# Two attention stages with their loops written out, fewer stack transfers, and new orders for SP and POOL

## What is computed

```python
x = x + attn(layernorm(x))        # 16 heads of width 16, relative positions
x = x + ffn(layernorm(x))         # a transformer layer: attention, then top-2 of 8 experts

# attn: distance of every query and key, clipped at +-64, picks a row of embK / embV
logits = einsum('bhqd,bhkd->bhqk', q, k) + einsum('bhqd,qkd->bhqk', q, embK[idx])
w = softmax(logits)
out = einsum('bhqk,bhkd->bhqd', w, v) + einsum('bhqk,qkd->bhqd', w, embV[idx])

# ffn, its attention: no relative positions
h = layernorm(x) * g + b
attn = softmax(q @ k.T / sqrt(16));  x = x + (attn @ v) @ w_o + b_o
# then layernorm, gate, and two of eight experts with 1024 hidden units a token
```

## Time and profile before

| | |
|---|---|
| median of 3 runs | 4886.3 us (4877.15 to 4907.61) |
| profiled execution | 4905.31 us, its span 4903.5 us |
| mean granted TensorE clock | 0.897 of full |
| relative attention, first to last collected head | 366.46 to 2376.10 us |
| plain attention, the same | 2749.21 to 4181.90 us |
| busy over the span | PE 85%, DVE 75%, ACT 61%, POOL 30% |

### The profile page before, as it was taken

The page is one execution under the profiler, slowest core; times in us unless marked ns, Lnnn a source line. Parts: engine busy times, 40 slices in busy tenths (PEclk is TensorE's granted clock), DMA queues, the critical chain, the costliest instruction groups (busy, mean ns, idle before and its releaser), DMA issues. The chain is left out here.

```text
span 4903.5 us, 90470 instructions
## 1 busy us (share of the span) xinstructions
PE 4163.6 (85%) x26888; PEld 2168.5 (44%) x26888; DVE 3684.1 (75%) x6647; ACT 3011.5 (61%) x5838; POOL 1451.2 (30%) x1418
## 2 busy tenths in 40 slices
PE   3769898989989898989655999999999999669997
PEld 1434444444444444444333333333333333469997
DVE  2678777787877777777357888888888888557775
ACT  0217777677767676767211578778778778236665
POOL 0025555465655555555300000000000000333332
PEclk9959998898989898989777899999999999779999
DMA  3656666566656666656545323223233322566664
GB/s 99 230 106 158 143 144 143 136 153 142 155 133 151 137 150 142 149 126 149 162 149 168 49 41 47 39 42 47 40 42 44 47 39 40 140 200 175 175 175 118
DMA packets 512569, 579.13 MB, mean 118 GB/s; under 512 B 71976, under 2 KB 451928, under 8 KB 502000
## 3 DMA queue, kind: packets, MB, share of 16 engines
q1 hardware_dynamic: 453568, 489.90, 44.7%
q10 hardware_dynamic: 38656, 58.73, 3.2%
q0 software_dynamic: 19824, 24.52, 3.2%
HBM read 365.10 MB, written 210.95 MB: 117 GB/s over the span
## 5 line engine op out<-in xcount | busy, mean ns | idle before, releaser
L1325 ACT ACTIVATE ra_p<-ra_psS 128x512 f32<-128x512 f32 x2051 | 1106.9, 604 | 565.7 <-PE ra_psS L1398 465.6
L633 DVE TENSOR_REDUCE pa_pm<-pa_psA 128x2 f32<-128x1024 f32 x1068 | 1261.6, 1220 | 175.5 <-PE pa_psA L724 175.3
L1232 DVE TENSOR_REDUCE ra_pm<-ra_psA 128x1 f32<-128x896 f32 x1072 | 1165.8, 1088 | 236.6 <-PE ra_psA L1358 179.8
L698 ACT ACTIVATE pa_p<-pa_psS 128x512 f32<-128x512 f32 x2054 | 1068.4, 602 | 287.3 <-PE pa_psS L747 264.9
L1358 PE MATMUL ra_psA<-ra_zs,ra_qs 48*128 48x512 f32 x2144 | 833.7, 479 | 179.7 <-DVE ra_rst L1251 113.5
L747 PE MATMUL pa_psS<-pa_qs,pa_zs 50*128 50x512 f32 x2056 | 807.5, 471 | 96.0 <-ACT pa_p L698 81.9
L724 PE MATMUL pa_psA<-pa_zs,pa_qs 48*128 48x512 f32 x2136 | 839.0, 477 | 50.5 <-DVE pa_recb L664 29.9
L1398 PE MATMUL ra_psS<-ra_qs,ra_zs 50*128 50x512 f32 (+3 forms) x2182 | 781.5, 439 | 48.4 <-ACT ra_p L1325 43.3
L747 PEld LDWEIGHTS pa_psS<-pa_qs,pa_zs 50*128 50x128 f32 x2056 | 349.0, 188 | 658.6 <-ACT pa_p L698 618.3
L1429 PE MATMUL ra_psO<-ra_p,ra_vs 128*32 128x512 f32 (+3 forms) x6400 | 600.9, 482 | 0.0
L1398 PEld LDWEIGHTS ra_psS<-ra_qs,ra_zs 50*128 50x128 f32 x2182 | 378.4, 200 | 451.2 <-ACT ra_p L1325 319.2
(11 more groups left out here) (250 smaller groups left out, 5295.2 us busy)
## 6 DMA issues: line engine op xcount, KB each, us to landing
relative_rows<-ra_rst SPq DMA_DIRECT2D x136, 512.0 KB, 5.1
ra_blk<-window_rows SPq DMA_DIRECT2D x128, 512.0 KB, 4.6
mo_w_raw<-ffn_W SPq DMA_DIRECT2D x58, 1024.0 KB, 5.6
ra_dl<-relative_rows SPq DMA_DIRECT2D x136, 256.0 KB, 4.2
window_rows<-ra_pc SPq DMA_DIRECT2D x128, 256.0 KB, 5.2
pa_qs<-q_halves SPq DMA_DIRECT2D x210, 128.0 KB, 5.6
pa_zs<-kl_halves SPq DMA_DIRECT2D x210, 128.0 KB, 6.9
ra_qs<-q_halves SPq DMA_DIRECT2D x204, 128.0 KB, 4.4
```

Source lines behind the costliest of these rows:

```text
L633: dve.reduce_max(pm[:, par, 2 * a:2 * a + 2], psA[w][:, :, :], AX.X).then_inc(s_am.h, 1)
L698: act.activation(pr[:, i % NPR, :], psS[:, slot(i), :], ACT.Exp).then_inc(s_ex.h, 1)
L1232: dve.reduce_max(pm[:, q, i, 2 * left:2 * left + 1], psA[w][:, lo:lo + 2 * G - P], AX.X).then_inc(s_far.h, 1)
L1325: act.activation(dst, psS[:, slot(i), :], ACT.Exp if kind == "E" else ACT.Copy).then_inc(s_cp.h, 1)
```

## The change

Four things change. In both attention stages the loops of SP, POOL, DVE and ACT are written out (all heads, waits on constants); the first pair of lines below stands for eight such pairs. `load_stack` uses five transfers for the same bytes, its rows in another order (the high and low rows of the keys alternate), for which `k_halves` holds both sides of the keys in one tensor and `e_stack` has the same order. `gather_denominators` uses one transfer for four, and the table `k_side` two for sixteen. SP's and POOL's orders in the relative stage are laid out anew, with other constants.

```diff
-            with sp.Fori(0, HEADS // U) as it:
+            for it in range(HEADS // U):
...
-for _c, _at in reversed(tuple(enumerate((38, 50, 59, 98)))):
+for _c, _at in reversed(tuple(enumerate((38, 53, 83, 88)))):
...
-WX_STEPS = (9, 10, 10, 10, 11, 11, 12, 13, 13, 15, 17, 18, 18, 18, 19, 20)
+WX_STEPS = (8, 10, 10, 10, 12, 13, 13, 14, 14, 14, 15, 17, 21, 22, 22, 23)
-REL_AHEAD, REL_LEAD = 16, 6
+REL_AHEAD, REL_LEAD = 18, 7
-RC_REL = 32
-SUM_TURNS = (8, 15, 24, 27)
+RC_REL = 30
+SUM_TURNS = (10, 17, 23, 28)
...
+                sp.dma_start(qs[at:two, w, :].bitcast(F32), bass.AP(qd.tensor, q0, [[T, DK], [0, 2], [1, S]])
+                             ).then_inc(done[w].h, 16)
+                sp.dma_start(qs[two:last, w, :].bitcast(F32), bass.AP(qd.tensor, q0 + D * T, [[T, DK], [1, S]])
+                             ).then_inc(done[w].h, 16)
+                for side in range(2):
+                    sp.dma_start(zs[at:two, w, side * far:(side + 1) * far].bitcast(F32),
+                                 bass.AP(kd.tensor, k0 + side * (D * T - 64), [[T, DK], [2 * D * T, 2], [1, far]])
+                                 ).then_inc(done[w].h, 16)
+                sp.dma_start(zs[two:last, w, 0:2 * far].bitcast(F32).rearrange("r (s c) -> r s c", s=2),
+                             bass.AP(kd.tensor, k0, [[T, DK], [D * T - 64, 2], [1, far]])).then_inc(done[w].h, 16)
...
+                sp.dma_start(den_d.rearrange("u (c q) -> c u q", c=4), ob[DK:P:32, :, :]).then_inc(s_dw.h, 16)
+                s_dw.wait(sp, 16 * (n + 1))
...
                 for p in range(U):
-                    load_stack(t + 1, p + 1, 64, s_qe, STEPS * t)
+                    if p == 2:
+                        load_v(t + 2, 4 * (t + 2))
                     write_r(t + 2, p, 0)
+                    write_r(t + 2, p, 1)
                     write_p(t, p, 0)
-                    write_r(t + 2, p, 1)
+                    write_p(t, p, 1)
                     read_p(t, p, 0)
                     read_r(t + 2, p, 0)
-                    write_p(t, p, 1)
+                    load_stack(t + 1, p + 1, 64, s_qe, STEPS * t)
+                    read_r(t + 2, p, 1)
                     write_r(t + 2, p, 2)
                     read_p(t, p, 1)
                     write_r(t + 2, p, 3)
-                    if p == 2:
-                        load_v(t + 2, 4 * (t + 2))
-                    read_r(t + 2, p, 1)
-                    read_r(t + 2, p, 3)
+                    write_p(t, p, 3)
                     write_p(t, p, 2)
                     if p % 2 == 0:
                         gather_denominators(t, n)
-                    write_p(t, p, 3)
+                    read_r(t + 2, p, 2)
                     read_p(t, p, 2)
-                    read_r(t + 2, p, 2)
+                    read_p(t, p, 3)
+                    read_r(t + 2, p, 3)
                     send_m(t + 1, p + 1)
-                    read_p(t, p, 3)
+                    if p % 2 == 0:
+                        spread_reciprocals(n)
                     s_am.wait(sp, 32 * (t + 2))
                     load_stack(t + 3, p + 1, 0, s_qa)
-                    if p % 2 == 0:
-                        spread_reciprocals(n)
                     if p % 2 == 0:
                         store_o(t, n)
...
                     t, n = U * it + p, 2 * it + p // 2
-                    lay_v(t + 1, p + 1, it + 1 + (p + 1) // U)
                     join_p(t, p, 0)
                     join_p(t, p, 1)
+                    lay_v(t + 1, p + 1, it + 1 + (p + 1) // U)
+                    fold_p(t, 0)
                     part_r(t + 2, 0)
-                    fold_p(t, 0)
                     join_p(t, p, 2)
                     join_p(t, p, 3)
+                    part_r(t + 2, 1)
                     fold_p(t, 1)
-                    part_r(t + 2, 1)
+                    part_r(t + 2, 2)
                     fold_p(t, 2)
                     fold_p(t, 3)
-                    part_r(t + 2, 2)
...
-                for hh in range(P // DK):
-                    sp.dma_start(k_side[hh * DK:(hh + 1) * DK, side:side + 1],
-                                 emb_k[r:r + 1, :].rearrange("r (d a) -> (r d) a", a=1)).then_inc(s_ld, 16)
+                row = emb_k[r:r + 1, :]
+                sp.dma_start(k_side[:, side:side + 1],
+                             bass.AP(row.tensor, row.offset, [[0, P // DK], [1, DK], [1, 1]])).then_inc(s_ld, 16)
```

More of the change, by code:

```diff
@@ L617, in _ @@
             lay_v(0, 0)
-            with pool.Fori(0, HEADS // U) as it:
+            for it in range(HEADS // U):
                 for p in range(U):
@@ L670, in _ @@
                     split_m(0, n % 2)
-            with dve.Fori(0, HEADS // U) as it:
+            for it in range(HEADS // U):
                 for p in range(U):
@@ L707, in _ @@
                 exp(0, i)
-            with act.Fori(0, HEADS // U) as it:
+            for it in range(HEADS // U):
                 for p in range(U):
@@ L933, in rel_attention @@
         blk = ctx.enter_context(nc.Block())
-        NLD = 16 * (len(Q2) + 2 * len(K2))
+        NLD = 16 * 5
         NINIT = 7
@@ L989, in load_stack @@
                 w = p % 2
-                row, col, col64 = ready(sp, h * DK), ready(sp, b * S), ready(sp, b * S + 64)
                 if free is not None:
                     s_us.wait(sp, free)
[L993 to L998, removed]
+                q0, k0 = qd.offset + h * DK * T + b * S, kd.offset + h * DK * T + b * S + 64
+                far, two, last = S - 64, at + 2 * DK, at + PR
+                sp.dma_start(qs[at:two, w, :].bitcast(F32), bass.AP(qd.tensor, q0, [[T, DK], [0, 2], [1, S]])
[8 more added lines that the diff above has]
+                             bass.AP(kd.tensor, k0, [[T, DK], [D * T - 64, 2], [1, far]])).then_inc(done[w].h, 16)
             def load_v(t, laid):
@@ L2412, in dram @@
         return nc.dram_tensor(name, shape, dt).ap()
-    q2, kl2, kr2 = (dram(n, (NP2, D, T)) for n in ("q_halves", "kl_halves", "kr_halves"))
+    q2 = dram("q_halves", (NP2, D, T))
+    k_sides = dram("k_halves", (NP2, 2, D, T))
+    kl2, kr2 = k_sides[:, 1, :, :], k_sides[:, 0, :, :]
     v_rows, f_rows = (dram(n, (T, D)) for n in ("v_rows", "f_rows"))
@@ L2461, in program @@
                               zero_fill=(zero, dr_p.rearrange("t (a i) q r -> (t a) i q r", a=4)))
-            rel_attention(nc, ident, sel, masks, q2, (kl2, kr2), v_rows, e_stack, evc, ev_side, dr_r, dr_p,
+            rel_attention(nc, ident, sel, masks, q2, k_sides, v_rows, e_stack, evc, ev_side, dr_r, dr_p,
                           den_d[0:UN, :], rec_d[0:UN, :], ot_rows)
```

16 lines of the change are left out of this document (5 added, 11 removed).

## The result

The changed kernel takes 4662.5 us (median of 4 runs, 4646.13 to 4681.83) against 4896.95 for the kernel before beside it: ratio 0.9523, 95% interval 0.9465 to 0.9581. The forecast was 4645, within 4605 to 4765; against the 4886.3 from which it counted that is a ratio of 0.9506, inside the interval. Its profiled execution took 4656.61 us where that of before took 4905.31: 248.7 us less, against the 241 of the sum.

The account below looks back on a forecast made before the run. Even relative heads were taken as PE-bound, the rest as losing time to loop jumps, SP's lateness and clock falls. -42 - 55 - 161 + 16 + 3 - 2 = -241 us gave a median of 4645 us, range 4605 to 4765.

Parts of the forecast that it names:

- The plain stage: Plain attention: without jumps, seven heads go from 49.7 to 43.7 us, 42 us won.
- The relative stage: Relative attention: 55 us from jumps in p = 3 heads and 161 us from SP's lateness, less charges.
- SP's lateness: Relative stage: SP's and POOL's late work after even heads lengthens odd heads; removing it wins 161 us, bounds 0 and 161.
- Is all of it removed?: Relative stage, SP's order: the first table write could leave 10 us earlier, where 4.7 were missing, so all lateness goes.
- all three waits: DVE's relative-stage waits for the `ra_rst` write (75.3 us), POOL's product (31.7) and stored results (20.3) should go.
- The charge of 16 us: Relative stage: late folds, tables or stacks stop PE, estimated at 0.5 us a head.
- The slacks: Relative stage, spare time in tightened links: 2.0 us for the table's chunk 0, 4 us for the A stack.
- The clock's share: Both stages: some 93 us of the gain is work at 1.2 GHz; a ramp bound would make the sum 44 us smaller.
- The +3 for two more A turns: Before the first relative head: two more A turns of 1.4 us stand ahead, costing 3 us.
- a wait under another name: Relative stage: chunk 0's table, A stack or fold some 3 us late in each head, giving 4754; chance 0.18.
- Only the written loops pay: Relative stage: odd heads stay at 66.7 us because something else holds SP's first write, giving 4790; chance 0.06.
- The table's chain: Relative stage: table work queues behind window writes and a fold; 8 us late gives 4962; chance 0.03 slower, 0.03 near nothing.

Follow-up runs that it names:

- Experiments 8: Changed kernel with the plain stage's loop restored on ACT alone: ratio 0.9554 to the kernel before, plain stage 1436.1 us.
- Kernel 12: Changed kernel with the plain stage's loops restored on SP, POOL and DVE, ACT's left written out: ratio 0.9477, plain stage 1387.9 us.
- experiment 3: Kernel before with both stages' loops written out, reciprocals moved ahead of the A stack's load and the fill stack behind the table writes: ratio 0.9782.
- kernel 6: Changed kernel with the old constants (REL_AHEAD, REL_LEAD, RC_REL, RING, WX_STEPS, SUM_TURNS): ratio 0.9573, relative stage 1846.3 us.
- 7: Kernel before with all loops written out and the new constants, but the old SP and POOL orders and nine transfers: ratio 0.9858, relative stage 1979.6 us.
- experiment 10: Changed kernel with the reciprocal two turns later (RC_REL 32 in place of 30): ratio 0.9527, relative stage 1823.7 us.
- 11: Kernel before with loops written out, SP's reciprocals and fill stack moved, and the reciprocal formed two turns earlier (RC_REL 30): ratio 0.9698, relative stage 1907.1 us.
- Experiments 5: Changed kernel with DVE's first sum of a head at turn 15 in place of 10: ratio 0.9418, 4615.5 us.
- kernel 9: Changed kernel with DVE's first sum of a head at turn 14 in place of 10: ratio 0.9371, 4590.0 us.
- experiment 4: Changed kernel with nine transfers a stack in place of five: ratio 0.948, 4649.12 us.
- kernel 2: Kernel before with the loops of both attention stages written out and nothing else: ratio 0.9754, 123.3 us faster.

## Why the prediction was right, point by point

**The plain stage: right.** -42 was forecast for the seven heads and -42.6 came; the 24 others gave 2 more. Experiments 8 and 12 narrow the step to ACT alone. The jump's direct cost is 2.6 or 2.7 us on average (18.1 / 7 and 18.8 / 7) of 6 to 7; the rest shows as PE's busy time (44.3 against 40.7 us a head), which is the clock, as the earlier trace rows had it. The Trainium skill, page "Runtime: NRT & Kernel Launch", section "Instruction fetch mechanics", says that a taken branch out of the sequencer's window stalls its engine for a fetch. ACT's wait of up to 2.9 us at each jump agrees with it, though no row here shows the fetch itself. Kernel 12, where three engines jump at no cost, shows that a jump counts only where it isn't covered.

**The relative stage: right in sum, and by kind of head.** Forecast were +8 for the even heads, -82 for p = 1, -126 for p = 3: they came as +8.3, -77.9 and -124.1, and the last head gave 8.9 in place of 1. Together -202.6 against -200. That it fits so closely is in part luck: the loops were under-sized (68 us by the profiles, 78 by the medians, not 55), SP's lateness, as what is then left, was over-sized (135 or 124 net of the charge, not 145), and profiles of one and the same relative stage differ by up to 29 us.

**What ends the lateness: credited too narrowly.** The step "Is all of it removed?" argued from SP's two moves, that the write could leave 10 us earlier and that "all three waits should go, and with them the clock's fall". The waits do go with those moves (experiment 3). The time doesn't: 29 + 13 waits of PE take their place. I had priced POOL's order and the constants as charges only, of 16 us. Kernels 6, 7, 10 and 11 show that they are what makes the moves pay: the reciprocal two turns earlier brings the A stack in time, and POOL's new order brings the folds in time only together with the new constants. Which of POOL's edits and which constant does it was not tried one by one, nor were SP's other moves.

**The charge of 16 us: its size fell right for even heads by luck, its mechanism was wrong.** It was to be late tables, stacks or folds. These waits came to 0.3 us. In their place stand the clock falls, some 50 us over the stage behind 0.9 us of idle time, which the prediction didn't name; the shortest heads are also 0.9 us below the 56.0 from which it counted, and that covered some 28 of the 50 (0.9 x 31). Experiments 5 and 9 show the place: take the sum out of it, and 54 us of PE's busy time come back.

**The slacks.** The A stack was given 4 us: it has about 1.6 (experiment 10). The timeline shows what was wrong in that sum. It let the 6.8 us of the landing start with the load, at 1031, and left out the issuing: the last of the five transfers leaves 2.5 us behind the first (962.72, 965.26), and it lands in 7.2 us. The load itself takes 3.0 us of SP, not the "5 x 0.44 = 2.2"; that cost no time, as experiment 4 shows that nine transfers do as well. The table's chunk 0 was given 2.0 us; DVE's wait for it doesn't occur in the stage, and how much is left wasn't measured.

**The clock's share.** Of the sum 93 us were to be work at 1.2 GHz coming back; by PE's busy time 61.0 + 25.0 = 86 did. The Trainium skill, page "TensorE: Matmul & The Clock Gate", section "Part 1: The HAM clock gate", puts the ramp penalty under 1% of a typical kernel's span. That sentence is on the warm-up at a kernel's start; the prediction stretched it to a bound on all falls of the clock. As such a bound the traces don't bear it out: those 86 us are 1.8% of the span of before, and kernel 9 takes back 54 more. To go by the rows was right, but the time alone would hardly tell: the forecast with the bound was 4689, 27 us above what was measured, where 4645 is 17 below.

**The small ones.** DVE's wait for `k_side` fell from 37.6 to 36.0, where 1 us was taken. The first collection came at 365.65 in place of 366.46. The +3 for two more A turns can't be told: with the same `REL_AHEAD` it came at 361.2 to 366.5 in kernels 4, 8, 10 and 12. All that lies outside the two stages is 1.2 us shorter.

**The rivals.** The first, a wait under another name, is real: kernel 3 is that case, and for the A stack the change misses it by some 1.6 us of slack. "Only the written loops pay" gave 4790, and kernel 2, which is just that, measured 4786, a fit by luck: 96 us were forecast as the gain and 123 measured, from a kernel before that took 4909.5 there. The change goes well beyond. The table's chain did not fall behind, and no ACT or DVE wait of the kind "issue" spreads over the heads.

## What to carry to other kernels

A wait behind a crowded queue goes when the order changes, but what was queued is then late somewhere else: before crediting a move, find the consumers of everything it steps past, and move their producers (here the reciprocal and POOL's folds) with it. Price idle time of TensorE by what the clock does behind it, and look for the place in a head where the granted clock falls: moving one operation of 0.7 us out of a 4 us stretch in which DVE is full was worth 1.6% here (0.9523 to 0.9371), where the merged transfers and the plain stage's loops of three engines were worth nothing that could be measured. Write out the loop of the engine whose jump isn't covered; in the plain stage the others could have kept theirs, in the relative stage that wasn't tried.

## What the runs showed of the hardware

- In the changed kernel the granted clock fell to 0.50 behind only 0.9 us of PE idle time in 4 us, no single gap of it over 0.5 us, always at the same place, in 17 heads of 31. In the other 14 it stayed at 1.00, and in the one shown PE's busy times before that point are the same to 0.01 us. What makes the difference between such heads stays open; with 0.5 us of idle time at this place (kernels 5 and 9) or 0.6 (kernel 6) it never fell there.
- A stack's merged transfers take SP 0.6 us each to issue, where the plain ones took 0.44 and 0.45 (kernel 4); merging nine to five saved 1 us of 4.
- A transfer of 16 KB (`reciprocals`) lands in 1.4 us when it isn't issued directly behind a stack's load, also in kernel 3, which still has nine transfers a stack. Issued directly behind one, in the kernel before, it took 7.2 us (count, KB, median us to landing, relative stage):

```profile
reciprocals<-ra_rec SPq DMA_DIRECT2D x16, 16.0 KB, 7.2
```
